# Local attention inside a four-stage block: full-depth score products and block-diagonal values in place of 32 by 32 products

## The chip, the cores and the metric

The kernel runs on one core of a Trainium2 chip. The time is the device time of one execution, in microseconds (us). The kernel before ran three times: 442.93, 444.45 and 447.99 us, median 444.45.

## The reference

The input is 8 batches of 256 tokens with 128 channels. Four stages run one after the other, each adding its result to x: a global causal attention with rotary positions, a feed-forward stage with blockwise FP4 rounding ("a"), the local attention that this change is about, and the feed-forward stage again ("b"). All arithmetic is float32. The local attention, cut to what matters:

```
xn = layernorm(x)                                     # over 128 channels
q, k, v = split(xn @ w_qkv, 3)                        # windows of LS = 32 tokens
q = rmsnorm(q, ln_w);  k = rmsnorm(k, ln_w)           # y * rsqrt(mean(y*y) + 1e-6) * ln_w
att = (q . k) / sqrt(8)                               # 16 heads of 8 channels, inside a window
att = softmax(where(causal, att, -max))
x = x + (att @ v) @ w_proj
```

A batch has 8 windows. Head h = 4g + j owns channels 32g + 8j to 32g + 8j + 7, with g (a group) and j from 0 to 3.

## The kernel before

Five instruction queues (TensorE "PE", VectorE "DVE", ScalarE "ACT", GpSimd "POOL", SyncE "SP" for DMAs) each run one in-order program. Every stage of every batch is written as a Python generator per engine (`front1` to `front3` for the global attention, `ffn1` to `ffn3` with w = `ffn_a` or `ffn_b`, `local1` and `local2` for the local attention). A `yield` ends a step, and the table `TIMES` gives each step its place; `weave` sorts the steps by it, so the order of each engine's instructions is written out beforehand (569 steps on PE, 406 on ACT, 617 on DVE, 119 on POOL, 40 on SP). `FFN_TURNS` says which feed-forward stage may next use the PSUM tile `ffb`. Stages of different batches overlap: while the global attention of one batch runs, the local and feed-forward stages of earlier ones are laid between its steps. Nothing is reordered at run time: an engine whose next instruction waits holds up everything behind it.

PSUM has three tiles: `fb` (four banks) for the global attention, `ffb` (two banks) for the feed-forward stages and `lb` (two banks of 512 float32 columns) for the local attention. So one batch at a time is in `lb`, from its first transpose to its last addition.

The local attention of a batch goes so (lines of the kernel before):

- ACT subtracts the mean (`centre`, L1062); the standard deviation isn't divided out, since the RMS norm removes a common factor from q and k. POOL works out that factor anyway (`deviation`, L1218 and L1220), for the values, and `evl` (L1242), which corrects the small constant of the RMS norm.
- PE transposes the tokens (L780), and multiplies by the weights of q and k (L910) and of v (L913: two products of 128 tokens by 128 channels). The weights of v have their sign turned once at the start (L1054).
- ACT squares and sums q and k (L1123), copies q to SBUF (L1025) and writes the values, scaled, to `Vl` with a column of ones behind each head (L1131). POOL makes the RMS factors `rql` (L1246, L1249). DVE scales k by its factor and the squared norm weights (L1421).
- PE transposes q and k (L780). ACT copies q to `qTl` and writes four copies of k to `Kd`, each with all channels zeroed but those of one j (L1138, a scale from the 0/1 mask `hm`).
- PE adds the causal mask (L927) and makes the scores with 32 products of 32 rows by 32 columns, each with 128 moving columns (L940), half of them in each of two steps.
- DVE takes the row maxima of both banks at once (L1430). PE subtracts them with two products of 512 columns (L946), since one scale per row is all that the exponential can take. ACT takes the exponential, one tile of 128 tokens after the other, with the factor of q as scale (L1149); DVE transposes in 32 by 32 blocks (L1436).
- PE multiplies by the values, 64 products per tile, each 32 rows by 32 columns with 9 moving columns (L960). A float32 product is two PE instructions, each with its own weight load, so this is 128 pairs per tile and 256 per batch. The first of them waits for both exponentials, because the result goes over scores of bank 0.
- DVE divides by the sums (L1440, L1443), PE transposes (L780) and projects (L969), DVE adds to x (L1446).

At the start PE, ACT and DVE wait for `consts_set`, which POOL raises after its last memset (L1203).

## Time and profile before

| | |
|---|---|
| median of 3 runs | 444.45 us |
| the profiled execution | 439.61 us, of which the span from first to last instruction is 437.8 us |
| mean granted TensorE clock | 0.858 of full speed |
| PE busy | 356.9 us, 82% of the span, 5005 matmul instructions |
| DVE busy | 272.3 us, 62% |
| ACT busy | 225.0 us, 51% |
| POOL busy | 149.6 us, 34% |

The busy time of an engine is the time in which at least one of its instructions ran; PE overlaps its matmuls, so a group's busy time is less than its count times the mean of one. PEld is the weight load that goes with each matmul. The granted clock is 1.0 at 2.4 GHz and 0.5 at 1.2 GHz.

### The profile page before, as it was taken

What the parts mean: (1) busy time and instruction counts of PE and PEld (TensorE: products, weight loads), DVE (VectorE), ACT (ScalarE), POOL (GpSimd) and SP (SyncE); (2) the same over time, 40 slices, a digit from 0 to 9 for tenths busy, and PEclk for the clock granted to TensorE, in tenths of its full rate; (3) what the DMA queues carried; (4) which work ended last, traced back from release to release, by engine and by line L of the source; (5) the groups of instructions that cost most, each with busy time, mean ns of one, the idle gap of its engine ahead of it and who ended that gap; (6) DMA issues with size and microseconds to landing.
All of it is one profiled execution on the core that took longest, in us unless ns stands there. A gap on an engine that the chain in (4) does not pass through costs nothing.

```text
span 437.8 us, 12067 instructions
## 1 busy us (share of the span) xinstructions
PE 356.9 (82%) x5005; PEld 236.8 (54%) x5005; DVE 272.3 (62%) x714; ACT 225.0 (51%) x583; POOL 149.6 (34%) x214
## 2 busy tenths in 40 slices
PE   3237799689798898989999999799999878878564
PEld 2124455456664675566566666566755645645333
DVE  2717207549678347867958956856866677654741
ACT  2310343264475348547647873578498476472421
POOL 4130124140451225136413540362460473332313
PEclk9755659599899958989999999779899999899665
DMA  6360062065000615001500150000000000000000
GB/s 180 95 126 0 4 146 72 19 141 86 4 3 3 146 40 108 1 7 36 106 10 18 46 97 4 3 1 3 18 1 1 15 3 1 15 12 3 13 13 12
DMA packets 33114, 17.67 MB, mean 40 GB/s; under 512 B 1874, under 2 KB 32914, under 8 KB 33060
## 3 DMA queue, kind: packets, MB, share of 16 engines
q1 hardware_dynamic: 32772, 16.78, 17.1%
q8 instruction: 39, 0.64, 0.6%
q10 hardware_dynamic: 288, 0.13, 0.1%
q14 instruction: 15, 0.12, 0.1%
HBM read 9.37 MB, written 7.34 MB: 38 GB/s over the span
## 4 chain that ended last, share of the span: by engine, by line
PE 53%; DVE 17%; ACT 12%; issue 7%; POOL 5%; DMA 3%; SPq 2%; DVEq 0%; POOLq 0%; ACTq 0%
PE fb L879 5%; DVE bmax L1371 4%; PE ffb L1011 4%; PE lb L960 4%; PE fb L797 3%; PE ffb L989 3%; PE ffb L993 3%; PE fb L836 3%; PE lb L946 3%; PE fb L867 3%; DMA Kf<-scr_f 3%; PE ffb L1005 2%; PE fb L838 2%; PE fb L869 2%; PE lb L780 2%
## 5 line engine op out<-in xcount | busy, mean ns | idle before, releaser
L1371 DVE TENSOR_REDUCE bmax<-fb 128x3 f32<-128x384 f32 x128 | 66.7, 548 | 27.9 <-PE fb L839 27.3
L1100 ACT ACTIVATE prob<-fb 128x384 f32<-128x384 f32 x128 | 59.5, 492 | 28.9 <-PE fb L870 28.3
L1270 POOL TENSOR_TENSOR fa__w<-fa__w,fa__c 128x704 f32<-128x704 f32 (+1 forms) x10 | 13.7, 1374 | 81.3 <-DVE fa__w L1500 81.3
L836 PE MATMUL fb<-Kf,Qf 48*128 48x256 bf16 x128 | 32.8, 301 | 10.4 <-DVE bmax L1371 4.9
L838 PE MATMUL fb<-maskb 64*128 64x256 bf16 x128 | 32.9, 301 | 0.0
L867 PE MATMUL fb<-Qf,Kf 51*128 51x256 bf16 x128 | 30.6, 298 | 1.2 <-ACT prob L1100 1.0
L879 PE MATMUL fb<-prob,Vf 128*32 128x128 f32 (+1 forms) x512 | 30.0, 356 | 1.1 <-ACT prob L1100 1.0
L869 PE MATMUL fb<-maskb 64*128 64x256 bf16 x128 | 30.3, 294 | 0.0
L960 PE MATMUL lb<-Vl,probT 32*32 32x9 f32 x2048 | 21.7, 175 | 7.0 <-issue 4.6
L836 PEld LDWEIGHTS fb<-Kf,Qf 48*128 48x128 bf16 x128 | 10.8, 95 | 27.9 <-DVE bmax L1371 16.5
L837 PE MATMUL fb<-Kf,Qf 48*128 48x128 bf16 x128 | 25.9, 235 | 0.0
L1270 POOL TENSOR_TENSOR fb__w<-fb__w,fb__c 128x704 f32<-128x704 f32 (+1 forms) x10 | 13.8, 1378 | 35.1 <-DVE fb__w L1500 35.1
L839 PE MATMUL fb<-maskb 64*128 64x128 bf16 x128 | 25.7, 233 | 0.0
L960 PEld LDWEIGHTS lb<-Vl,probT 32*32 32x32 f32 x2048 | 19.8, 107 | 10.8 <-issue 7.8
L868 PE MATMUL fb<-Qf,Kf 51*128 51x128 bf16 x128 | 24.2, 232 | 0.0
L797 PE MATMUL fb<-xnTf,wT 128*128 128x256 f32 x64 | 22.7, 516 | 1.5 <-ACT xnTf L1025 1.5
L870 PE MATMUL fb<-maskb 64*128 64x128 bf16 x128 | 23.8, 228 | 0.0
L879 PEld LDWEIGHTS fb<-prob,Vf 128*32 128x32 f32 x512 | 14.2, 115 | 16.4 <-issue 7.4
L1229 POOL TENSOR_TENSOR qk<-ra,rb 128x512 f32<-128x512 f32 x7 | 8.9, 1269 | 39.2 <-DVE rb L1352 39.2
L1025 ACT ACTIVATE oTf<-fb 128x256 f32<-128x256 f32 x32 | 12.3, 385 | 16.9 <-PE fb L879 16.8
L867 PEld LDWEIGHTS fb<-Qf,Kf 51*128 51x128 bf16 x128 | 10.2, 95 | 19.0 <-issue 10.9
L1011 PE MATMUL ffb<-wdT,fb__hqT 128*128 128x128 f32 (+1 forms) x96 | 17.0, 326 | 3.9 <-ACT fb__hqT L1025 3.9
(202 smaller groups left out, 939.4 us busy)
## 6 DMA issues: line engine op xcount, KB each, us to landing
scr_f<-partsf SPq DMA_DIRECT2D x16, 192.0 KB, 2.4
Qf<-scr_f SPq DMA_DIRECT2D x16, 192.0 KB, 3.8
...
```

The source lines that it names most:

```text
L797: mm = pe.matmul(fb[:, n // 2, (n % 2) * SEQ:(n % 2 + 1) * SEQ], wT[:, n, :], xnTf[:, :], start=True, stop=True)
L836: pe.matmul(S[:, 128:384], Qf[k, g, 128:256], Kf[k, g, 0:256], start=True, stop=True, skip_group_check=True)
L837: pe.matmul(S[:, 0:128], Qf[k, g, 0:128], Kf[k, g, 0:128], start=False, stop=True, skip_group_check=True)
L838: pe.matmul(ends(S, 0, 128), eye_lo[half_, :], twice(m_qk[half_, :]), start=False, stop=True, skip_group_check=True)
L867: pe.matmul(S[:, 128:384], Kf[k, g, 0:128], Qf[k, g, 0:256], start=True, stop=True, skip_group_check=True)
L869: pe.matmul(two(S[:, 0:256], 0, 128), eye_hi[half_, :], twice(m_kq[half_, :]), start=False, stop=True, skip_group_check=True)
L879: mm = pe.matmul(S[32 * j:32 * j + 32, k * P:SEQ], Vfs[b % RING][:, k, h, :], p, start=(k == 0), stop=(k == 1), skip_group_check=True)
L960: mm = pe.matmul(lb[rows, 0, (t * H + h) * VL:(t * H + h + 1) * VL], probT[rows, t, c // 4, c % 4 * LS:(c % 4 + 1) * LS], Vl[rows, t, h, : ...
L1011: mm = pe.matmul(ffb[:, t, 0:D], w.hqT[0:k, t, c, :], wdT[0:k, c, :], start=(c == 0), stop=(c == 2))
L1100: act.activation(prob[:, slot % 8, :], S[:, 0:384], ACT.Exp).then_inc(f.s_exp, 1)
L1270: pool.tensor_tensor(w.w[:, cols], w.w[:, cols], w.c[:, cols], ALU.subtract).then_inc(w.s_hdif, t1 - t0)
L1371: dve.tensor_reduce(bmax[:, h, 1:4], fb[:, h % 2, 0:384].rearrange("p (n k) -> p n k", k=P), AX.X, ALU.max).then_inc(bmax_done, 1)
```

## The change

The score rows are laid out anew: a partition is now (j, query) of one window and a column (window of the tile, g, key), so all 16 heads of a window come out of one product of full depth. Tile t of 128 tokens has bank t of `lb` for its scores and its results.

- ACT writes four masked copies of q (`Qd`, mask `hm`) and four of k (`Kd`, new mask `quarter`, which keeps one group of 32 channels), eight in all in place of one and four.
- PE makes the scores of a window in one product, 128 deep, 128 by 128: 8 per batch in place of 32. Mask, maxima, subtraction, exponential and values go by tile: the second half of the scores doesn't wait behind other work, each tile has its own maxima (two reductions of 512), and the values of tile 0 no longer wait for the exponential of tile 1.
- The values are block-diagonal (`Vd`): row (j, key), four blocks of 9 columns, of which one isn't zero. So 4 groups and 4 windows make 16 products per tile, each 128 deep, 32 by 36: 32 per batch in place of 128. To have the values in rows (j, key), the value projection is 32 products of 32 tokens by 32 channels in place of 2, and ACT writes `Vd` in four masked copies of 256 columns in place of two of 128.
- The layer norm now divides by the deviation: DVE makes a shift (`shl`) and ACT's first step waits for it, which waits for POOL's factor. POOL's `evl` goes. The factor of q moves from the exponential to the copy of q (two ACT instructions in place of one), which now waits for POOL's `rql`.
- At the start ACT's turn of the sign of v goes, and POOL clears `Vd` and sets its ones (one memset of 1152 columns and four of 32 partitions) in place of one small memset.
- `FFN_TURNS` and the whole table `TIMES` are written anew: 577 steps on PE, 414 on ACT, 633 on DVE, as many as before on POOL and SP. In the start, DVE's four steps on the feed-forward weights now come ahead of the rotary products of batch 0, and SP issues one load of x ahead of the first loads of Q and K, not four.

The rest of the kernel is the same line for line. The diff without the tables, the buffers and the launch:

```
-"ident": np.concatenate([eye, (r[:, None] % LS // HD == np.arange(4)[None, :])], 1).astype(np.float32),
+"ident": np.concatenate([eye, r[:, None] % LS // HD == np.arange(4)[None, :], r[:, None] // LS == np.arange(4)[None, :]], 1).astype(np.float32),
...
+Kd = sb("Kd", [P, T * NWIN, GROUPS, LS])
+Qd = sb("Qd", [P, T * NWIN, 4, LS])
+Vd = sb("Vd", [P, T * NWIN, GROUPS, 4, VL])
+nmaxl = sb("nmaxl", [P, T, NWIN * GROUPS])
...
-    for t in range(T):
-        mm = pe.matmul(lb[:, 1, SEQ + t * D:SEQ + (t + 1) * D], xnTl[:, t * P:(t + 1) * P], wqkvb[:, 2 * D:3 * D], start=True, stop=True)
+    wv = wqkvb[:, 2 * D:3 * D].rearrange("p (g j d) -> p j g d", j=4, d=HD)
+    for w in range(T * NWIN):
+        for j in range(4):
+            mm = pe.matmul(lb[j * LS:(j + 1) * LS, 1, SEQ + w * LS:SEQ + (w + 1) * LS], xnTl[:, w * LS:(w + 1) * LS], wv[:, j, :, :],
+                           start=True, stop=True, skip_group_check=True)
     mm.then_inc(l.s_qkv_ps, 1)
...
-    pe.wait_ge(l_kd, b + 1)
-    for i in range(2):
-        pe.matmul(lb[:, i, :], identb, mask_loc.unsqueeze(1).to_broadcast([P, 2, T * P]), start=True, stop=True, skip_group_check=True)
-    for gg in range(2):
-        c0 = gg * T * P
-        if gg:
-            mm.then_inc(l_half, 1)
-            yield
-            pe.wait_ge(l_half, b + 1)
-        for t in range(T):
-            for n in range(NWIN):
-                k0 = t * P + n * LS
-                for i in range(2):
-                    g = 2 * gg + i
-                    rows = slice(32 * g, 32 * g + 32)
-                    mm = pe.matmul(lb[n * LS:(n + 1) * LS, i, c0 + t * P:c0 + (t + 1) * P], qTl[rows, k0:k0 + LS],
-                                   Kd[rows, :, k0:k0 + LS], start=False, stop=True, skip_group_check=True)
-    mm.then_inc(l.s_sc_ps, 1)
-    yield
-    pe.wait_ge(l.s_nmax, b + 1)
-    for i in range(2):
-        mm = pe.matmul(lb[:, i, :], identf, nmaxl[:, 16 * i:16 * i + 16].unsqueeze(2).to_broadcast([P, 16, LS]),
-                       start=False, stop=True, skip_group_check=True)
-    mm.then_inc(l_mx_ps, 1)
-    yield
+    pe.wait_ge(l_qd, b + 1)
     for t in range(T):
         if t:
             yield
-        else:
-            pe.wait_ge(l.s_exp, T * (b + 1))
+        pe.matmul(lb[:, t, :], identb, mask_loc.unsqueeze(1).to_broadcast([P, 2, T * P]), start=True, stop=True, skip_group_check=True)
+        for n in range(NWIN):
+            w = t * NWIN + n
+            mm = pe.matmul(lb[:, t, n * P:(n + 1) * P], Qd[:, w, :, :].rearrange("p j q -> p (j q)"), Kd[:, w, :, :].rearrange("p g k -> p (g k)"),
+                           start=False, stop=True, skip_group_check=True)
+        mm.then_inc(l.s_sc_ps, 1)
+    for t in range(T):
+        yield
+        pe.wait_ge(l.s_nmax, T * b + t + 1)
+        pe.matmul(lb[:, t, :], identf, nmaxl[:, t, :].unsqueeze(2).to_broadcast([P, 16, LS]),
+                  start=False, stop=True, skip_group_check=True).then_inc(l_mx_ps, 1)
+    for t in range(T):
+        yield
         pe.wait_ge(l_probT, T * b + t + 1)
-        for c in range(H):
-            h = 4 * (2 * (c // 4 % 2) + c // 8) + c % 4
+        for g in range(GROUPS):
             for n in range(NWIN):
-                rows = slice(n * LS, (n + 1) * LS)
-                mm = pe.matmul(lb[rows, 0, (t * H + h) * VL:(t * H + h + 1) * VL], probT[rows, t, c // 4, c % 4 * LS:(c % 4 + 1) * LS],
-                               Vl[rows, t, h, :], start=True, stop=True, skip_group_check=True)
+                mm = pe.matmul(lb[n * LS:(n + 1) * LS, t, g * 4 * VL:(g + 1) * 4 * VL], probT[:, t, n, g * LS:(g + 1) * LS],
+                               Vd[:, t * NWIN + n, g, :, :].rearrange("p j e -> p (j e)"), start=True, stop=True, skip_group_check=True)
     mm.then_inc(l.s_o_ps, 1)
...
-    act.wait_ge(lnw_loaded, 48)
-    act.activation(wqkvb[:, 2 * D:3 * D], wqkvb[:, 2 * D:3 * D], ACT.Copy, scale=-1.0)
...
-    centre(l, b, xnl, mvl)
+    act.wait_ge(l_sh, b + 1)
+    for t in range(T):
+        ins = act.activation(xnl[:, t, :], xall[:, b, t, :], ACT.Identity, scale=rsl[:, 1, t:t + 1], bias=shl[:, t:t + 1])
+    ins.then_inc(l.s_xn, 1)
     yield
     act.wait_ge(l.s_xnT_ps, b + 1)
     copy(xnTl[:, :], lb[:, 1, 0:SEQ]).then_inc(l.s_xnT, 1)
...
             ins = act.activation(sql[:, 2 * a + t, :], q4[:, t, a, :], ACT.Square, scale=D ** -0.5,
                                  accum_out=ssl[:, 2 * a + t:2 * a + t + 1])
     ins.then_inc(l_ss, 1)
-    copy(qkn[:, 0, :, :], q4[:, :, 0, :]).then_inc(l_q, 1)
+    yield
+    act.wait_ge(l_rms, b + 1)
+    for t in range(T):
+        ins = act.activation(qkn[:, 0, t, :], q4[:, t, 0, :], ACT.Copy, scale=rql[:, 1, t:t + 1])
+    ins.then_inc(l_q, 1)
     yield
     act.wait_ge(l.s_qkv_ps, 2 * b + 2)
-    act.wait_ge(l.s_rstd, 2 * b + 2)
-    for t in range(T):
-        ins = act.activation(Vl[:, t, :, 0:HD], lb[:, 1, SEQ + t * D:SEQ + (t + 1) * D].rearrange("p (h d) -> p h d", h=H), ACT.Copy,
-                             scale=rsl[:, 1, t:t + 1])
+    v = lb[:, 1, SEQ:2 * SEQ].rearrange("p (n d) -> p n d", d=HD)
+    for j in range(4):
+        ins = act.activation(Vd[:, :, :, j, 0:HD].rearrange("p w g d -> p (w g) d"), v, ACT.Copy, scale=quarter[:, j:j + 1])
     ins.then_inc(l.s_v, 1)
     yield
     act.wait_ge(l_qkT_ps, b + 1)
-    copy(qTl[:, :], lb[:, 1, 0:SEQ])
+    for g in range(GROUPS):
+        act.activation(Kd[:, :, g, :], lb[:, 1, SEQ:2 * SEQ].rearrange("p (w k) -> p w k", k=LS), ACT.Copy, scale=quarter[:, g:g + 1])
     for j in range(4):
-        ins = act.activation(Kd[:, j, :], lb[:, 1, SEQ:2 * SEQ], ACT.Copy, scale=hm[:, j:j + 1])
-    ins.then_inc(l_kd, 1)
+        ins = act.activation(Qd[:, :, j, :], lb[:, 1, 0:SEQ].rearrange("p (w q) -> p w q", q=LS), ACT.Copy, scale=hm[:, j:j + 1])
+    ins.then_inc(l_qd, 1)
     yield
 def local2(b):
     yield
-    act.wait_ge(l_mx_ps, b + 1)
-    s5 = lb[:, :, :].rearrange("p i (g t k) -> p (i g) t k", g=2, t=T)
     for t in range(T):
         if t:
             yield
-        act.activation(probl[:, t, :, :], s5[:, :, t, :], ACT.Exp, scale=rql[:, 1, t:t + 1]).then_inc(l.s_exp, 1)
+        act.wait_ge(l_mx_ps, T * b + t + 1)
+        act.activation(probl[:, t, :, :].rearrange("p n k -> p (n k)"), lb[:, t, :], ACT.Exp).then_inc(l.s_exp, 1)
     yield
     act.wait_ge(l.s_aT_ps, b + 1)
     copy(attnTl[:, :], lb[:, 1, 0:SEQ]).then_inc(l.s_aT, 1)
...
-    pool.memset(Vl[:, :, :, HD:HD + 1], 1.0).then_inc(consts_set, 1)
+    pool.memset(Vd[:, :, :, :, :].rearrange("p w g j e -> p (w g j e)"), 0.0).then_inc(pool_chain, 1)
+    pool.wait_ge(pool_chain, RING + 1)
+    for j in range(4):
+        ins = pool.memset(Vd[j * LS:(j + 1) * LS, :, :, j, HD:VL].rearrange("p w g e -> p (w g) e"), 1.0)
+    ins.then_inc(consts_set, 1)
...
     deviation(b, l, mvl, rsl)
-    pool.tensor_tensor(evl[:, :], rsl[:, 0, :], eps[:, 1, 0:T], ALU.mult).then_inc(l_ev, 1)
     yield
     pool.wait_ge(l_ss, b + 1)
-    pool.wait_ge(l_ev, b + 1)
-    pool.tensor_tensor(rql[:, 0, :].rearrange("p (a t) -> p a t", a=2), ssl[:, :].rearrange("p (a t) -> p a t", a=2),
-                       evl[:, :].unsqueeze(1).to_broadcast([P, 2, T]), ALU.add).then_inc(l_sscale, 1)
+    pool.tensor_tensor(rql[:, 0, :], ssl[:, :], eps[:, 1, :], ALU.add).then_inc(l_sscale, 1)
     pool.wait_ge(l_sscale, b + 1)
     pool.tensor_tensor(rql[:, 1, :], rql[:, 0, :], half[:, :], ALU.pow).then_inc(l_rms, 1)
...
     yield
+    dve.wait_ge(l.s_rstd, 2 * b + 2)
+    if b > 0:
+        dve.wait_ge(l.s_xn, b)
+    dve.scalar_tensor_tensor(out=shl[:, :], in0=mvl[:, :, 0], scalar=-1.0, in1=rsl[:, 1, :], op0=ALU.mult, op1=ALU.mult).then_inc(l_sh, 1)
+    yield
     dve.wait_ge(l_rms, b + 1)
     dve.wait_ge(l_q, b + 1)
     if b == 0:
...
     yield
-    dve.wait_ge(l.s_sc_ps, b + 1)
-    dve.tensor_reduce(nmaxl[:, :], lb[:, :, :].rearrange("p i (n k) -> p (i n) k", k=LS), AX.X, ALU.max, negate=True).then_inc(l.s_nmax, 1)
+    for t in range(T):
+        if t:
+            yield
+        dve.wait_ge(l.s_sc_ps, T * b + t + 1)
+        dve.tensor_reduce(nmaxl[:, t, :], lb[:, t, :].rearrange("p (n k) -> p n k", k=LS), AX.X, ALU.max, negate=True).then_inc(l.s_nmax, 1)
     yield
     for t in range(T):
         if t:
...
     yield
     dve.wait_ge(l.s_o_ps, b + 1)
-    o = lb[:, 0, 0:T * H * VL].rearrange("p (h e) -> p h e", e=VL)
-    link(chain, dve.reciprocal(rdenl[:, :], o[:, :, HD]))
+    o = lb[:, :, 0:H * VL].rearrange("p t (h e) -> p t h e", e=VL)
+    link(chain, dve.reciprocal(rdenl[:, :].rearrange("p (t h) -> p t h", t=T), o[:, :, :, HD]))
     yield
     linked(chain)
-    dve.tensor_tensor(attnl[:, :, :], o[:, :, 0:HD], rdenl[:, :].unsqueeze(2).to_broadcast([P, T * H, HD]), ALU.mult).then_inc(l.s_attn, 1)
+    dve.tensor_tensor(attnl[:, :, :].rearrange("p (t h) d -> p t h d", t=T), o[:, :, :, 0:HD],
+                      rdenl[:, :].rearrange("p (t h) -> p t h", t=T).unsqueeze(3).to_broadcast([P, T, H, HD]), ALU.mult).then_inc(l.s_attn, 1)
     yield
     dve.wait_ge(l.s_proj_ps, b + 1)
```

## Rows read from the trace of the kernel before

**Rows 1.** Page, part 1: busy us (share of span) and instructions.
```profile
PE 356.9 (82%) x5005; PEld 236.8 (54%) x5005; DVE 272.3 (62%) x714; ACT 225.0 (51%) x583; POOL 149.6 (34%) x214
```
**Rows 2.** Windows: length, busy us of PE, PEld, DVE, ACT, POOL; granted clock; DMA.
```profile
120.00:360.00 240.00, 220.71 (x3579) 148.24 (x3574) 169.63 (x456) 151.06 (x409) 93.00 (x130) 0.94 0.14 31
360.00:410.00 50.00, 39.36 (x783) 26.57 (x782) 32.02 (x76) 25.91 (x63) 16.74 (x22) 0.92 0.03 10
410.00:437.80 27.80, 14.78 (x46) 9.83 (x46) 11.06 (x30) 6.94 (x15) 8.30 (x12) 0.56 0.03 10
```
**Rows 3.** Page, part 4: the chain that ended last, by engine.
```profile
PE 53%; DVE 17%; ACT 12%; issue 7%; POOL 5%; DMA 3%; SPq 2%; DVEq 0%; POOLq 0%; ACTq 0%
```
**Rows 4.** Groups of PE: line, tiles, forms, count | busy us, mean ns | idle before.
```profile
L960 PE MATMUL lb<-Vl,probT 32*32 32x9 f32 x2048 | 21.7, 175 | 7.0 <-issue 4.6 <-DVE probT L1436 2.3
...
L913 PE MATMUL lb<-wqkvb,xnTl 128*128 128x128 f32 x32 | 5.0, 279 | 0.0
```
**Rows 5.** Timeline of PE: start us, length us, line, count, idle before.
```profile
147.54 1.25 PE L960 MATMUL lb<-Vl,probT 32*32 32x9 f32 x128
148.72 1.09 PE L886 MATMUL fb<-identhm,oTf 128*128 128x128 f32 x8
...
153.12 1.04 PE L960 MATMUL lb<-Vl,probT 32*32 32x9 f32 x63 [2.00 <-issue]
...
175.55 0.67 PE L940 MATMUL lb<-Kd,qTl 32*32 32x128 f32 x32
176.15 0.28 PE L836 MATMUL fb<-Kf,Qf 48*128 48x256 bf16 x1
...
180.13 0.86 PE L879 MATMUL fb<-prob,Vf 128*32 128x256 f32 x16
180.92 0.28 PE L867 MATMUL fb<-Qf,Kf 51*128 51x256 bf16 x1
...
403.07 1.60 PE L1011 MATMUL ffb<-wdT,fb__hqT 128*128 128x128 f32 x12
404.61 0.55 PE L960 MATMUL lb<-Vl,probT 32*32 32x9 f32 x46
```
**Rows 6.** Windows around the stall at 151 us, columns as in rows 2.
```profile
151.10:153.10 2.00, 0.02 (x3) 0.00 (x0) 0.00 (x0) 0.00 (x0) 0.00 (x0) 0.98 0.50 71
153.50:166.50 13.00, 13.00 (x115) 9.88 (x109) 6.76 (x26) 6.54 (x17) 4.11 (x9) 0.50 0.15 40
```
**Rows 7.** Timeline of ACT in the last batch's local attention.
```profile
385.98 0.40 ACT L1025 ACTIVATE qkn<-lb 128x256 f32<-128x256 f32 x1
386.24 0.65 ACT L1131 ACTIVATE Vl<-lb,rsl 128x128 f32<-128x128 f32 x2
386.74 0.91 ACT L1025 ACTIVATE fb__hqT<-ffb 128x384 f32<-128x384 f32 x2
...
390.02 1.56 ACT L1138 ACTIVATE Kd<-lb,identhm 128x256 f32<-128x256 f32 x4
391.44 0.41 ACT L1025 ACTIVATE fb__xqT<-ffb 128x256 f32<-128x256 f32 x1
```
**Rows 8.** Timeline of all engines, the same batch: maxima, subtraction, exponential.
```profile
396.49 1.23 DVE L1430 TENSOR_REDUCE nmaxl<-lb 128x32 f32<-128x1024 f32 x1 [0.52 <-PE lb L940]
397.77 1.99 PE L946 MATMUL lb<-nmaxl,identhm 128*128 128x512 f32 x4 [0.60 <-DVE nmaxl L1430]
399.79 1.26 ACT L1149 ACTIVATE probl<-lb,rql 128x512 f32<-128x512 f32 x2 [2.12 <-PE lb L946]
```
**Rows 9.** Timeline of all engines at the start.
```profile
3.33 0.95 POOL L1198 MEMSET Vf<- 128x1024 f32 x1
...
4.57 0.15 POOL L1203 MEMSET Vl<- 128x32 f32 x1
4.76 0.49 DVE L1326 BATCH_NORM_STATS2 stf<-xall 128x6 f32<-128x128 f32 x2 [2.73 <-POOL Vl L1203]
...
20.09 0.68 DVE L1363 TENSOR_TENSOR partsf<-restf,partsf 128x512 bf16<-128x512 f32 x1
```

503 lines of the change are left out of this document (246 added, 257 removed), and 97 rows, old and new, of tables (FFN_TURNS, TIMES).

## The prediction, made before the changed kernel ran

> **What bounds the kernel now.** I read part 1 first, for which engine carries the load [rows 1]: PE is busy for 82% of the span, DVE for 62, ACT for 51. Then windows, because such shares are means over stages [rows 2]. From 120 to 360 us PE is busy for 220.7 of 240 us (92%), DVE for 71%, ACT for 63%: here PE bounds. From 360 to 410 us PE has 79% and works for the last two local attentions, which lie one after the other in `lb`: here the length of that chain counts as much. After 410 us only the last feed-forward stage is left. The chain of waits agrees [rows 3]: PE 53%, DVE 17%, ACT 12%, issue 7%.
>
> So the change is worth what it takes from PE in the middle, what it takes from the chain through `lb` near the end, less what its new work on ACT gives back. The sum is made against the profiled execution, 439.61 us; the median of the three runs is 4.84 us (1.1%) above it. I add the sum to the median.
>
> **Part by part, per batch, then times 8.** I price PE by slots: from the start of a burst to the start of the next work behind it. A burst's own length has the latency of its last product in it, and that lies under what follows.
>
> Scores. Before: 64 instructions (32 float32 products) have a slot of 0.60 us for each half, 175.55 to 176.15 [rows 5], with one half in each step; that makes 1.20 us. After: 8 products of full depth, 16 instructions of 128 by 128 with 128 columns. That form stands at L1011, 12 in 1.54 us, 0.128 us each [rows 5], so 2.05 us. The new scores cost 0.85 us more, +6.8 us in all: the small products overlapped in the array, and full ones can't. Mask and subtraction have the same columns as before and cost nothing new.
>
> Values. Before: 128 pairs of load and product in 1.18 us, 147.54 to 148.72 [rows 5], 9.2 ns a pair, twice per batch: 2.36 us. After: 64 pairs, 128 deep, 32 wide, with 36 columns. No row has this form. One neighbour is L960 itself with 9 columns. The other has the new one's depth and width: L879, 16 instructions of which half have 256 and half 128 columns, in 0.79 us, 49 ns each at 192 columns on average [rows 5]. A straight line between 9 and 192 columns gives 15 ns at 36. I take this, 0.97 us, a gain of 1.39 us, -11.1 us in all. Lower end: 9.2 ns, 0.59 us, -14.2. Upper end: no overlap between products, each 36/128 of 0.128 us, so 36 ns, 2.3 us, -0.5.
>
> Value projection. Before 5.0 us in 8 batches, 0.62 us each with about 0.17 us of latency in it [rows 4]. After: 64 pairs with 32 columns; the same line gives 14 ns, 0.91 us, so +0.46 us, +3.7 us in all. Lower end +1.1, upper end (32 ns each) +12.8.
>
> So PE's slots come to -0.6 us, between -6.3 and +19.1. The three quarters fewer value products are mostly paid for by the other two. L879 speaks against the upper end: without overlap its 16 instructions would take 16 x 1.5 x 0.128 = 3.1 us, and they take 0.79.
>
> Stalls inside a burst. The value products are the only matmuls here that use up instructions faster than 10 ns a pair, and the one group with long idle time that nothing but issue ends: 4.6 us of 7.0 [rows 4]. One stall alone is 2.00 us, at 151.1, in the middle of a burst [rows 5], with DVE, ACT and POOL at rest as well [rows 6]. PE's local instructions fall from 2624 to 1184 pairs (2048, 512 and 32 + 32 before; 512, 128 and 512 + 32 after, L910 being the same). I take three quarters of the stalls as gone, -3.5 us; ends 0 and -4.6.
>
> The clock. Behind that stall the granted clock goes to 0.50, the 1.2 GHz level, for 13 us from 153.5, in which PE is never idle [rows 6]; at 2.4 GHz that work would take 6.5 us. I take half, -3.5 us; ends 0 and -6.5, since the first idle time that the new order makes can do the same.
>
> Waits in `lb`. PE's idle time before the values that ends with a DVE transpose is 2.3 us [rows 4]. The values of tile 0 no longer wait for both exponentials; -1.0 us, ends -2.3 and +1.
>
> ACT. A plain copy of 256 columns holds ACT for 0.26 us (385.98 to 386.24), the two value copies for 0.50 (to 386.74), a scaled copy of 256 for 0.355 (four in 1.42 us, 390.02 to 391.44) [rows 7]. Masked q and k: 8 x 0.355 - 0.26 - 1.42 = +1.16 us. Values: 4 x 0.355 - 0.50 = +0.92. q in two scaled pieces: 0.50 - 0.26 = +0.24. The exponential loses its scale operand, at best -0.1. That is +2.2 us a batch, 17.6 us in all. What hides it is the 37% that ACT is idle while PE bounds [rows 2]; if that cover were gone, all 17.6 would show. What does queue behind the steps of 2.84 us (masks) and 1.42 us (values) are exponentials of the global attention, for which PE waits two steps later. I charge ACT's part in the chain and a little for the blocks, 17%: +3.0 us.
>
> DVE. One reduction of 1.23 us [rows 8] becomes two of 512, some 0.7 each, and the shift is a tiny operation of about 0.2: +0.35 us a batch; at DVE's 17% of the chain +0.4 us in all. POOL loses one tiny operation: nothing.
>
> The start. POOL's memset of 1024 columns takes 0.95 us, and DVE's first operation waited for the last one, at 4.57 [rows 9]. 1152 columns take 1.07 us and the small ones follow: `consts_set` is 1.4 us later. But batch 0 goes on only when the third part of q and k is there, at 20.09 us [rows 9], behind the weights' steps on DVE and ACT, which wait for their own DMA; and these are now ahead in DVE's order. I take +0.5, ends -1 and +1.4. SP issues three loads fewer ahead of the first Q and K: nothing, since those wait for the scratch's writes.
>
> The chain through `lb` in the last two batches. Longer: v's four copies stand between q's and the transposes (+1.4 us), three more masked copies (+1.2 us), and ACT's first step waits for POOL and DVE, which the wait for `lb` hides. Shorter: with a tile per bank the second maxima, subtraction and exponential overlap. Before, 1.23, 1.99 and 1.26 us follow one another [rows 8]; after, half of each lies beside the other tile's, some 2.1 us. Net +0.5 us for each batch, +1.0.
>
> Sum: -0.6 - 3.5 - 3.5 - 1.0 + 3.0 + 0.4 + 0.5 + 1.0 = -3.7 us, rounded to -4: 435.6 for a profiled execution, 440.5 for the median. The new order as a whole has no term; I give it 4 us either way.
>
> **The rivals.**
>
> 1. The gain is larger. The pair's spacing stays at 9.2 ns (slots -6.3), all stalls go (-4.6) and so does the slow stretch (-6.5), with -1.0 and +4.9 as above: -13.5, 431 us. For: bursts half as long. Against: the clock is also low where no value product is near, as at the end, 0.56 [rows 2]. Chance 0.20.
> 2. Slower: ACT becomes what the exponentials wait for. Place: ACT's queue between 120 and 360 us, at the masked copies. Price: all of the 17.6 us in place of 3.0, so +10.9, 455 us. It decides once PE finds both score banks full at each such block; ACT's load there goes from 63% to about 70%. Chance 0.15.
> 3. Slower: products of 32 columns have a floor. If 128 x 32 tiles didn't overlap as L879's do, the slots would be +19.1 in place of -0.6: +16, 460 us; the place is L913's and L960's successors. Half way there, 24 ns a pair, gives +9.5 for the slots and 451 us. The row against it is the pair of 9.2 ns, though at a quarter of the depth. Chance 0.10. The Trainium skill, TensorE: Matmul & The Clock Gate, section "Wait — 56ns, not 53.3ns?", says that matmuls never start closer than about 25 ns, however few columns they have; by that rule this rival's half-way case would be the result. The trace of before disagrees at least for 32 x 32 tiles.
> 4. The stalls aren't a matter of how many instructions there are, and the clock falls elsewhere: -3.7 + 3.5 + 3.5 = +3.3, 448 us. That the DMA engines were half busy in the 2 us stall [rows 6] speaks for it, against it that the long stalls lie inside value bursts. Chance 0.13.
>
> **The numbers.** Forecast 0.42, by itself 436 to 445 us. A measurement of this kernel can tell about 1% from no change, 440.0 to 448.9 us. Faster: half of the forecast, all of rival 1, a little of the others, 0.43. Same: the other half, most of rival 4, 0.32. Slower: rivals 2 and 3 and the rest, 0.25. The range reaches to rival 1 and to the half-way case of rival 3: 430 to 452 us.
>
> **What would show it.** Slots of the new value burst near 1.0 us, of the value projection near 0.9, of a tile's four score products near 1.0 (with the mask 1.2). PE's idle time by issue before the values under 1 us. ACT busy near 243 us, DVE near 275, PE near 356. Half-clock stretches fewer between 120 and 400 us. I would be wrong if PE's busy time fell by over 10 us, if ACT's wait ended PE's idle time by over 8 us more than before, or if the new order moved the last local attention by more than the terms above.

## The result, and the profile after

The changed kernel takes 423.01 us (median of 4 runs, 422.21 to 423.25); the kernel before took 443.69 in the same session. The ratio is 0.956, 95% interval 0.949 to 0.964: 20.7 us faster, where 440.5 was forecast, with 430 as the lower end. The profiled execution takes 422.98 us (span 421.1), 16.6 less than that of before. Some executions of a kernel take over 1.5% longer than its fastest; the ratios, and the medians from here on, leave them out (442.9 us for the kernel before).

Part 1 of the page and the chain of waits, to be read beside [rows 1] and [rows 3]:

```profile
PE 337.3 (80%) x3565; PEld 221.1 (53%) x3565; DVE 281.3 (67%) x730; ACT 242.4 (58%) x630; POOL 149.5 (36%) x210
...
PE 42%; DVE 18%; ACT 17%; issue 11%; DMA 5%; SPq 4%; POOL 3%; DVEq 0%; POOLq 0%; ACTq 0%
```

PE is busy for 19.6 us less, where 0.9 was forecast; ACT (242.4) is where it was forecast and DVE (281.3) is 6 us above. PE's share of the chain falls from 53% to 42%, ACT's rises from 12% to 17%. The windows answer to [rows 2]:

```profile
120.00:360.00 240.00, 217.88 (x2551) 144.29 (x2550) 186.22 (x487) 172.75 (x458) 92.67 (x125) 0.96 0.14 30
360.00:410.00 50.00, 32.50 (x298) 21.55 (x296) 28.39 (x79) 23.04 (x60) 15.59 (x22) 0.81 0.03 9
```

In the middle PE is nearly as full as before (91% and 92%), with 2551 matmul instructions in place of 3579. The groups of the three changed products, against [rows 4], and one burst of each with the work that follows it, against [rows 5]:

```profile
L938 PE MATMUL lb<-Kd,Qd 128*128 128x128 f32 x128 | 17.4, 280 | 0.0
...
L951 PE MATMUL lb<-Vd,probT 128*32 128x36 f32 x512 | 7.0, 201 | 1.1 <-DVE probT L1438 1.1
L918 PE MATMUL lb<-wqkvb,xnTl 128*32 128x32 f32 x512 | 6.1, 199 | 0.0
```
```profile
145.36 0.47 PE L951 MATMUL lb<-Vd,probT 128*32 128x36 f32 x32
145.76 0.44 PE L782 MATMUL fb<-identhm,attnf 128*128 128x128 f32 x2
...
207.92 1.05 PE L938 MATMUL lb<-Kd,Qd 128*128 128x128 f32 x8
208.90 0.28 PE L869 MATMUL fb<-Qf,Kf 51*128 51x256 bf16 x1
...
277.59 0.76 PE L918 MATMUL lb<-wqkvb,xnTl 128*32 128x32 f32 x64
278.28 0.86 PE L984 MATMUL ffb<-wguT,fa__xqT 128*128 128x352 f32 x2
```

A tile's 32 value pairs have a slot of 0.40 us, its scores one of 0.9 to 1.0, the 64 pairs of the value projection one of 0.69. The idle time before the values is 1.1 us in all, where [rows 4] had 7.0, and issue ends none of it. No gap of PE over 0.15 us that only issue ends is left anywhere in the trace of after; before had 6.7 us of them. (In the chain, where all engines count, issue rises from 7% to 11%.)

I also read when the global attention of each batch ends (the start, in us, of the DVE addition that closes it), since that work bounds the middle of the kernel. The lower lines are experiments, explained below.

| kernel | batch 0 | 1 | 2 | 3 | 4 | 5 | 6 | 7 |
|---|---|---|---|---|---|---|---|---|
| before | 76.0 | 114.1 | 157.0 | 209.6 | 242.6 | 277.9 | 313.8 | 350.2 |
| after | 77.4 | 108.8 | 147.7 | 186.7 | 227.5 | 262.1 | 298.8 | 333.9 |
| e5 (before, short value bursts) | 74.0 | 112.0 | 152.3 | 202.2 | 233.5 | 269.1 | 303.2 | 339.3 |
| e1 (old work, new order) | 78.7 | 110.2 | 152.2 | 200.5 | 244.7 | 284.6 | 328.2 | 366.6 |
| e9 (the same, short value bursts) | 77.9 | 109.5 | 149.9 | 192.2 | 230.2 | 266.1 | 308.3 | 342.4 |
| e12 (value copies on POOL) | 78.7 | 110.1 | 149.6 | 190.2 | 238.1 | 272.1 | 310.8 | 346.9 |
| e15 (the same, later in POOL's queue) | 77.4 | 108.9 | 147.7 | 186.8 | 224.5 | 259.1 | 297.6 | 333.8 |

From batch 7 to the end both kernels take some 87 us, so the 16 us are won before that. The most is won in batch 3, which takes 52.6 us before and 39.0 after (49.9 in e5, 42.3 in e9); batch 4 gives a part of it back, with 33.0 us before and 40.8 after.

### The profile page after: what moved, and what is told of

Read it like the earlier page. It is cut to its first block, busy times and chain, and to the rows that moved or that the text cites. A ratio compares the mean times of both kernels' runs of the same rounds, so it can differ in the third digit from the quotient of the medians.

```text
span 421.1 us, 9229 instructions
## 1 busy us (share of the span) xinstructions
PE 337.3 (80%) x3565; PEld 221.1 (53%) x3565; DVE 281.3 (67%) x730; ACT 242.4 (58%) x630; POOL 149.5 (36%) x210
## 4 chain that ended last, share of the span: by engine, by line
PE 42%; DVE 18%; ACT 17%; issue 11%; DMA 5%; SPq 4%; POOL 3%; DVEq 0%; POOLq 0%; ACTq 0%
PE fb L881 4%; PE fb L838 4%; PE fb L799 3%; DVE bmax L1365 3%; PE ffb L1002 3%; ACT prob L1088 3%; DMA Kf<-scr_f 3%; PE ffb L980 3%; PE fb L869 2%; PE ffb L984 2%; PE fb L840 2%; PE lb L938 2%; PE ffb L996 2%; PE fb L888 2%; PE lb L944 2%
## 5 line engine op out<-in xcount | busy, mean ns | idle before, releaser
L838 PE MATMUL fb<-Kf,Qf 48*128 48x256 bf16 x128 | 31.3, 300 | 12.2 <-DMA Kf<-scr_f 7.9
L840 PE MATMUL fb<-maskb 64*128 64x256 bf16 x128 | 31.3, 299 | 0.0
L881 PE MATMUL fb<-prob,Vf 128*32 128x128 f32 (+1 forms) x512 | 28.8, 344 | 2.5 <-ACT prob L1088 2.4
L871 PE MATMUL fb<-maskb 64*128 64x256 bf16 x128 | 30.5, 287 | 0.0
L838 PEld LDWEIGHTS fb<-Kf,Qf 48*128 48x128 bf16 x128 | 10.4, 94 | 32.0 <-DVE bmax L1365 16.3
L839 PE MATMUL fb<-Kf,Qf 48*128 48x128 bf16 x128 | 24.7, 234 | 0.0
L841 PE MATMUL fb<-maskb 64*128 64x128 bf16 x128 | 24.4, 232 | 0.0
L872 PE MATMUL fb<-maskb 64*128 64x128 bf16 x128 | 24.1, 224 | 0.0
L799 PE MATMUL fb<-xnTf,wT 128*128 128x256 f32 x64 | 21.7, 498 | 2.1 <-ACT xnTf L1016 2.1
L1227 POOL TENSOR_TENSOR qk<-ra,rb 128x512 f32<-128x512 f32 x7 | 8.9, 1267 | 38.4 <-DVE rb L1346 38.4
L799 PEld LDWEIGHTS fb<-xnTf,wT 128*128 128x128 f32 x64 | 15.5, 253 | 7.1 <-ACT xnTf L1016 4.1
L1002 PEld LDWEIGHTS ffb<-wdT,fb__hqT 128*128 128x128 f32 (+1 forms) x96 | 14.7, 233 | 7.5 <-ACT fb__hqT L1016 6.8
L1016 ACT ACTIVATE oTf<-fb 128x256 f32<-128x256 f32 x32 | 12.2, 381 | 10.5 <-PE fb L881 10.3
```

Source lines behind the costliest of these rows:

```text
L799: mm = pe.matmul(fb[:, n // 2, (n % 2) * SEQ:(n % 2 + 1) * SEQ], wT[:, n, :], xnTf[:, :], start=True, stop=True)
L838: pe.matmul(S[:, 128:384], Qf[k, g, 128:256], Kf[k, g, 0:256], start=True, stop=True, skip_group_check=True)
L839: pe.matmul(S[:, 0:128], Qf[k, g, 0:128], Kf[k, g, 0:128], start=False, stop=True, skip_group_check=True)
L840: pe.matmul(ends(S, 0, 128), eye_lo[half_, :], twice(m_qk[half_, :]), start=False, stop=True, skip_group_check=True)
L841: mm = pe.matmul(ends(S, 64, 64), eye_hi[half_, :], twice(m_qk[half_, 0:64]), start=False, stop=True, skip_group_check=True)
L871: pe.matmul(two(S[:, 0:256], 0, 128), eye_hi[half_, :], twice(m_kq[half_, :]), start=False, stop=True, skip_group_check=True)
```

## The experiments

All times are medians; a ratio is to the kernel before in the same session with its 95% interval. "After" stands at 0.956 [0.949, 0.964]. The median of all runs of the kernel before was 445.9 us in the session of e1 to e4, 444.1 in that of e5 to e8, 443.2 for e9 to e12 and 441.9 for e13 to e15, so ratios of different sessions can differ by 0.9% more than their intervals say. Where two experiments are compared, I give the difference of the medians.

### The order and the work, crossed: e1, e2

e1 is the kernel before with the places of the steps, and the turns of `ffb`, of the kernel after; e2 is the other way round. Steps that one of them lacks are merged with or put behind a neighbour; 5 and 13 steps had to move by a place or more, since the mix would have waited for itself.

```
-TIMES, FFN_TURNS of before      +TIMES, FFN_TURNS of after, two-tile steps merged      (e1)
-TIMES, FFN_TURNS of after       +TIMES, FFN_TURNS of before, new steps 0.1 behind      (e2)
```

> The kernel before, instruction for instruction, but with the new kernel's order of steps and feed-forward turns (the steps that only the new kernel has are left out of the list; 5 of 1950 steps stand one place earlier, so that no engine waits for a step behind the one that waits). Theory A, the gain is in the new local attention's instructions: 437 to 448 us. Theory B, the gain is in the new order of all stages, most of it between 77 and 187 us where the two profiles part: 424 to 431 us. The term for the order in the prediction was 4 us either way.

> The new local attention with the order of steps and the feed-forward turns of the kernel before (its added steps stand right beside the old ones they came from; 13 steps stand one or two places earlier, so that no engine waits for a step behind the one that waits). Theory A, the new instructions carry the gain whatever the order: 423 to 430 us. Theory B, the order carries it: 438 to 446 us. If both parts are needed together, both this run and the old work in the new order are above 436 us.

Measured: e1 467.85 us, ratio 1.046 [1.041, 1.051]; e2 495.93 us, ratio 1.112 [1.104, 1.120]. Both mixes are slower than either theory had them, so the case holds in which both parts are needed together. Each work is best in its own order, by 25 and by 73 us. So the new table is no gain that one can take alone. What in the work it fits is the question of e5, e9, e13 and e14.

### The number of value pairs: e3, e8, e10

These are the kernel after, with each value product cut into pieces. Operands, results and order stay.

```
-                        for n in range(NWIN):
-                            mm = pe.matmul(lb[..., g * 4 * VL:(g + 1) * 4 * VL], probT[...], Vd[:, t * NWIN + n, g, :, :]...)
+                        for j in range(4):           # e3; e8: range(2), 18 columns each; e10: 4 in tile 0, 1 in tile 1
+                            for n in range(NWIN):
+                                mm = pe.matmul(lb[..., (g * 4 + j) * VL:(g * 4 + j + 1) * VL], probT[...], Vd[:, t * NWIN + n, g, j, :], ...)
```

> The new kernel with each value product of 36 columns issued as four products of 9 columns with the same 32-wide weights: as many pairs of load and product per tile (128) as in the kernel before, same result, same order. Theory A1, the number of instructions in a value burst is what cost the time before (long bursts run out of instructions, PE stops, the clock falls): bursts of 1.2 us again, stalls in them, 6 to 15 us slower than the new kernel, 429 to 438 us. Theory A2, only the bursts' own length counts: 2 x 8 x 0.75 us of PE at most, 0 to 6 us slower. Theory B, the order carries the gain: the same as A2.

> The new kernel with each value product issued as two of 18 columns, same result: 64 pairs per tile and 128 per batch, between the new kernel's 32 and 64 and the kernel before's 128 and 256. With four pieces the slots of the group grew by about 20 us, of which some 10 are stalls that came after 200 to 250 pairs close together. If those stalls need that many pairs in a row: no stall of over 0.3 us, only the longer slots, 2 to 7 us slower than the new kernel, 425 to 430 us. If stalls grow in proportion to the pairs: half of the 24 us, 433 to 437 us.

> The kernel after, with the 128 short value pairs of e3 in tile 0 only; tile 1 keeps its 32. The result is the same. By a sum over pairs this is half of e3's extra work, 768 pairs: half of e3's 26 us, 436 us. If what costs is that PE runs out of instructions behind some 200 pairs in a row, a burst of 128 with 32 behind it never gets there: PE has no stall of 2 us inside or behind the values, and the time is the slots alone, 0.8 us a batch, 429 us or less. If one burst of 128 is enough for the stall, 440 or more.

| | pairs per tile | us | ratio |
|---|---|---|---|
| after | 32, 32 | 423.0 | 0.956 [0.949, 0.964] |
| e8 | 64, 64 | 423.9 | 0.962 [0.953, 0.970] |
| e10 | 128, 32 | 429.5 | 0.969 [0.964, 0.974] |
| e3 | 128, 128 | 448.7 | 1.015 [1.009, 1.020] |

The pairs alone take the whole gain away: e3 is as slow as the kernel before, or a little slower, and slower than any of its theories had it. The groups of e8, then of e3, and a part of e3's timeline on PE:

```profile
L952 PE MATMUL lb<-Vd,probT 128*32 128x18 f32 x1024 | 11.4, 187 | 0.8 <-DVE probT L1439 0.4 <-issue 0.3
```
```profile
L952 PE MATMUL lb<-Vd,probT 128*32 128x9 f32 x2048 | 21.5, 179 | 9.6 <-issue 9.4 <-DVE probT L1439 0.2
```
```profile
221.02 2.32 PE L952 MATMUL lb<-Vd,probT 128*32 128x9 f32 x250
225.55 0.24 PE L952 MATMUL lb<-Vd,probT 128*32 128x9 f32 x6 [2.21 <-issue]
225.72 0.87 PE L997 MATMUL ffb<-identhm,fa__hq 128*128 128x128 f32 x6
...
265.65 1.50 PE L881 MATMUL fb<-prob,Vf 128*32 128x256 f32 x15 [2.35 <-issue]
...
347.34 1.83 PE L952 MATMUL lb<-Vd,probT 128*32 128x9 f32 x196
351.31 0.68 PE L952 MATMUL lb<-Vd,probT 128*32 128x9 f32 x60 [2.15 <-issue]
```

Where both tiles' bursts lie one behind the other, PE stops for 2.2 us after 250 pairs, and after 196 in another batch. e3 has seven gaps inside its bursts, 0.3 to 2.2 us long, 9.4 us in all, and two more of 3.6 us together behind a burst (one is the line at 265.65): 13.0 us that only issue ends. A burst of 128 pairs has a slot of 1.19 us in e3, against 0.40 for 32, so 16 bursts cost 12.6 us. The two together are 25.6 of the 26 us. e8, with half the pairs, has two gaps, 0.3 and 0.7 us: its stalls are not half of e3's, and neither is its loss (0.9 us in place of 26, less than its expectation had).

e10 is less clean. PE's timeline of e10, behind a burst and inside one:

```profile
332.04 1.55 PE L954 MATMUL lb<-Vd,probT 128*32 128x9 f32 x160
333.52 0.44 PE L782 MATMUL fb<-identhm,attnf 128*128 128x128 f32 x2
333.79 0.38 PE L999 MATMUL ffb<-identhm,fa__hq 128*128 128x128 f32 x2
335.50 0.33 PE L999 MATMUL ffb<-identhm,fa__hq 128*128 128x128 f32 x1 [1.33 <-issue]
...
395.62 0.32 PE L954 MATMUL lb<-Vd,probT 128*32 128x36 f32 x12 [1.69 <-issue]
```

Its slots cost half of the 12.6 us, 6.3. Its expectation had the time (429 us or less, 429.5 measured), but not the reason: PE does stop, once for 1.7 us after 148 pairs in a row and four times for 0.5 to 1.3 us within 3 us behind a burst, 4.9 us in all. Slots and stops add up to 11.2 us where 6.5 were measured, so a part of the stops doesn't reach the end. The mean granted clock of the profiled runs of after and e3 is the same, 0.92, so the clock doesn't make the difference between these two.

### Short value bursts in the old work: e5, e9

In both orders, the old value products with 16 per tile in place of 64, each with the 36 columns of four heads (for three heads of every four the result is wrong):

```
-                    for c in range(H):
-                        h = 4 * (2 * (c // 4 % 2) + c // 8) + c % 4
+                    for c in range(0, H, 4):
+                        h = 4 * (2 * (c // 4 % 2) + c // 8)
...
-                            ... (t * H + h + 1) * VL], probT[rows, t, c // 4, c % 4 * LS:(c % 4 + 1) * LS], Vl[rows, t, h, :], ...
+                            ... (t * H + h + 4) * VL], probT[rows, t, c // 4, 0:LS], Vl[rows, t, h:h + 4, :]..., ...
```

> The kernel before, in its own order, with 16 value products per tile in place of 64: each is still 32 by 32 but moves the 36 columns of four heads, with the probabilities of the first of them (the other three heads' results are wrong). So it has the new kernel's number of value instructions and columns, and nothing else of it. Theory A, long bursts of value instructions and the stalls in them were the cost: the group's slots fall from about 26 us in all to 7, and most of it reaches the end even in the old order: 424 to 434 us. Theory B, the order decides and gives back only what it was made for: 437 to 446 us.

> The kernel of e1 (the instructions of before in the order of after), but with 16 value products of 36 columns per tile in place of 64 of 9, as in e5 (three heads of every four get a wrong result). With e5, before and e1 this makes a table of two orders by two kinds of value burst. Theory: the new order leaves room for short value bursts only, so the short bursts bring far more here than the 12 us of e5: under 450 us, 20 us or more below e1's 468. Rival: the misfit of e1 lies in the other durations and waits (one maximum over both tiles, the half scores, one masked copy of q), and the short bursts bring their 12 us as in the old order: 456 us or more.

Measured: e5 429.6 us, ratio 0.980 [0.965, 0.995]; e9 436.04 us, ratio 0.989 [0.980, 0.998].

| median us | old order | new order |
|---|---|---|
| old work, 128 value pairs per tile | 442.9 | 467.9 (e1) |
| old work, 32 pairs | 429.6 (e5) | 436.0 (e9) |
| new work, 128 pairs | not run | 448.7 (e3) |
| new work, 32 pairs | 495.9 (e2) | 423.0 (after) |

The short bursts bring 13 us in the old order (9 by the ratio) and 32 in the new one. The groups of e1 and of e9:

```profile
L960 PE MATMUL lb<-Vl,probT 32*32 32x9 f32 x2048 | 23.7, 180 | 16.3 <-issue 9.3 <-ACT probl L1149 6.5 <-DVE probT L1436 0.4
```
```profile
L960 PE MATMUL lb<-Vl,probT 32*32 32x36 f32 x512 | 7.1, 199 | 7.6 <-ACT probl L1149 6.5 <-DVE probT L1436 1.0
```

16.6 us of busy time and all 9.3 us of issue go, 26 of the 32; the wait for the exponential, which tiles of their own end in the kernel after, stays at 6.5. With short bursts the old work gains nothing from the new order (429.6 and 436.0 us, with ratios whose intervals overlap). With long ones it loses 25 us by it; in the new order the bursts of two tiles lie close together, and 9.3 us of issue stand in e1's trace against 6.7 in that of before. PE's waits for ACT are 34.4 us in e1 against 19.4, and they stay in e9 (37.9), so the stops are not the whole of e1's loss.

### The order of the start: e6

The kernel before with after's places for the first stages (43 steps on PE, 42 on DVE, 30 on ACT, 10 on SP differ), the rest as before.

> The kernel before, instruction for instruction, with the new kernel's order for the first stages alone: the weights, the global attention of batches 0 and 1 and its first part of batches 2 and 3, the loads of x, and the first steps of the first feed-forward stage (43 of 569 steps of PE differ, 30 on ACT, 42 on DVE, 10 on SP). No local attention runs there. In the profiles the global attention of batch 1 takes 38.1 us before (76.0 to 114.1) and 31.5 us after (77.4 to 108.8), and so it does in both runs with exchanged orders, by the order. Theory B, the order gains 6 us there by itself: batch 1 ends at 108 to 110 us and the whole is 4 to 7 us faster than before. Theory A (what is gained there is lost again, because the steps behind stand in the old order): batch 1 ends early, the whole within 2 us of before.

Measured: 440.9 us, ratio 0.996 [0.988, 1.003], no difference that can be told. The execution that was traced took 974 us, so this run has no milestones. The global attention of batch 1, with no local work beside it, takes 31.5 us in every kernel with the new order (after, e1, e9) and 38 in those with the old one (before, e5, e2, by the table of milestones and e2's 38.4). So 6.6 us come from the order there. The whole of e6 isn't faster by them: either the old order behind them loses them again or they never came about in e6, which can't be read without its trace.

### ACT's new work: e4, e7, e13, e14

```
+                for g in range(GROUPS):                              # e4: eight more, into tiles that nobody reads
+                    act.activation(Kx[:, :, g, :], lb[:, 1, SEQ:2 * SEQ]..., ACT.Copy, scale=quarter[:, g:g + 1])
+                for j in range(4):
+                    act.activation(Qx[:, :, j, :], lb[:, 1, 0:SEQ]..., ACT.Copy, scale=hm[:, j:j + 1])
...
-                for g in range(GROUPS):                              # Kd, Qd, Vd: 4, 4, 4 copies
+                for g in range(GROUPS if b == 0 else 2):             # e7: 2, 2, 4;  e13, e14: 1, 2, 2
```

> The new kernel with eight more masked copies per batch on ACT, of the same size and source, into two tiles (bfloat16) that nobody reads, ahead of the eight that count: ACT is held 2.8 us longer per batch, 23 us in all, and the chain through lb is that much longer. If ACT's new work is hidden as far as the prediction took it (17% of it shows): 3 to 6 us slower. If it is what now bounds: over 12 us slower. If it costs nothing: within 2 us of the new kernel.

> The new kernel with four of the eight masked copies per batch from batch 1 on (two of k, two of q; the other tiles keep batch 0's content, so the result is wrong). ACT has 1.42 us less per batch, 10 us in all, and the chain through lb is as much shorter. If the new kernel is bound by ACT and this chain throughout: 8 to 13 us faster, 410 to 415 us. If its order hides what it was made for, and only delays show: 0 to 4 us faster, 419 to 423 us.

> The kernel after, in its own order, but from batch 1 on with one of the four masked copies of k, two of q and two of v (the others keep batch 0's data, so the result is wrong): 7 copies of 0.36 us a batch less, which takes ACT's busy time back to that of before, some 225 us. This measures the ACT term of the sum (+3.0 us by the prediction, all 17.6 by its rival 2). By the prediction's 17%: 420 us. By e7 (6.5 us for 10): 411 or 412. If every microsecond of ACT shows: 406.

> The kernel of e2 (the work of after in the order of before, 496 us), with the same 7 copies left out from batch 1 on. Theory: what the old order has no room for is ACT's new work, so the mix loses its price: 450 us or less, 45 us or more below e2, where the same cut in the new order (e13) brings some 12. Rival: the old order is as badly off with the other new steps (a shift and a factor to wait for ahead of the layer norm, a step for each tile): 480 us.

| | ACT busy, us | us | ratio |
|---|---|---|---|
| e4 | 264.6 | 454.5 | 1.018 [1.014, 1.023] |
| after | 242.4 | 423.0 | 0.956 [0.949, 0.964] |
| e7 | 232.6 | 416.6 | 0.947 [0.939, 0.955] |
| e13 | 226.1 | 417.8 | 0.949 [0.942, 0.955] |
| e2, new work in the old order | 244.9 | 495.9 | 1.112 [1.104, 1.120] |
| e14, the same with less ACT | 227.9 | 476.1 | 1.079 [1.068, 1.090] |

The tiles that e7, e13 and e14 leave out keep batch 0's content. Going down, the first 10 us of ACT give 6.5 (4.2 by the ratios) and the next 6.5 nothing; both results lie between the cases of their expectations. Going up, 22 us cost 31, by the medians and between the profiled executions alike. There is no one rate for ACT's work: the order has room for what it was written for, and above it every microsecond and more shows. e4's copies stand ahead of those that count and so lengthen the chain through `lb` as well; load and chain aren't told apart here. In the old order the same 16 to 17 us are worth 20, and the mix stays 33 us slower than before. PE's waits in e14, by what it waited for (total, times, longest):

```profile
PE lb L782 <- ACT xnl L1104: 8.1, 4, 3.6
PE lb L782 <- DVE attnl L1445: 7.0, 4, 2.9
PE ffb L1002 <- ACT fb__hqT L1016: 6.4, 7, 2.8
PE fb L869 <- ACT prob L1088: 5.8, 6, 1.6
```

The largest is the transpose that waits for the scaled layer norm (2.7 us in after, 0.8 before), which now has POOL's factor and DVE's shift ahead of it; that these steps lie too close together in the old order is my reading. My theory for e14 (that ACT's copies are all that doesn't fit) fell; the rival's 480 came within 4 us.

### The value projection: e11

```
-                for w in range(T * NWIN):
-                    for j in range(4):
-                        mm = pe.matmul(lb[j * LS:(j + 1) * LS, 1, SEQ + w * LS:SEQ + (w + 1) * LS], xnTl[:, w * LS:(w + 1) * LS], wv[:, j, :, :], ...)
+                for t in range(T):
+                    mm = pe.matmul(lb[:, 1, SEQ + t * D:SEQ + (t + 1) * D], xnTl[:, t * P:(t + 1) * P], wqkvb[:, 2 * D:3 * D], start=True, stop=True)
```

> The kernel after with the old value projection, two products of 128 by 128 in place of 32 of 32 by 32 (the values then stand in the wrong rows, so the result is wrong). The prediction charged the 32 small products 3.7 us. Their slot after is 0.69 us against some 0.5 for the two, so by slots 1 to 2 us are to be had: 421.5 us. By the prediction's term 419. If the 64 instructions also eat into what PE has in stock, more: 415.

Measured: 417.92 us, ratio 0.945 [0.940, 0.951], some 5 us less than after, between the term of the prediction (3.7) and the dearest case. Its slots are 0.44 to 0.54 us in place of 0.69, 1.6 us in all. The trace doesn't say where the other 3 come from.

### The value copies on POOL: e12, e15

ACT copies v once, POOL writes the four masked copies in one operation, and PE's values wait for it. In e15 that step is 1 to 5 places later in POOL's queue in six of the batches.

```
+                    pool.wait_ge(l.s_v, b + 1)
+                    pool.tensor_tensor(Vd[:, :, :, :, 0:HD]..., vl[:, :]... (each value four times), quarter[:, :]... (each mask along the values), ALU.mult).then_inc(l_vd, 1)
...
-                    for j in range(4):
-                        ins = act.activation(Vd[:, :, :, j, 0:HD]..., v, ACT.Copy, scale=quarter[:, j:j + 1])
+                    copy(vl[:, :], lb[:, 1, SEQ:2 * SEQ]).then_inc(l.s_v, 1)
```

> The kernel after, but ACT copies the values once to SBUF (0.26 us in place of 4 x 0.36) and POOL writes the four masked copies in one operation of 1024 columns (some 2.4 us by the 1.27 us of its 512-column sums), two steps later in its queue; PE's values wait for it. ACT loses about 9 us, POOL gains 19. By e7 (6.5 us for 10 us of ACT) the time falls to 417 or 418. If POOL's block of 2.4 us delays the feed-forward stages or the rotary sums behind it, the gain is eaten: 423 to 428. By the prediction's 17% for ACT's work: 421.5.

> The kernel of e12 (the four masked copies of v on POOL, one operation of 1.9 us), with POOL's new step one to five places later in its queue in six of the batches, so that it no longer stands ahead of the rotary sums (batch 2, where e12 lost most) or of a feed-forward step. ACT's load is the same as in e12. If e12's loss of 14 us against after was the place in the queue: 417 to 420 us, better than after. If it is POOL's 15 us of work or a slower POOL and DVE beside each other: 430 or more.

Measured: e12 435.8 us, ratio 0.986 [0.979, 0.993], slower than every case of its expectation; e15 424.62 us, ratio 0.963 [0.955, 0.971]. e15 lies between its two cases. The load is the same in both (ACT 234.3 and 233.4, POOL 164.3 and 164.5 us). POOL's timeline in e12, and the same stretch in e15:

```profile
191.27 1.26 POOL L1230 TENSOR_TENSOR qk<-ra,rb 128x512 f32<-128x512 f32 x1
195.45 1.89 POOL L1252 TENSOR_TENSOR Vd<-vl,identhm 128x1024 f32<-128x1024 f32 x1 [2.92 <-ACT vl L1020]
197.30 1.15 POOL L1233 TENSOR_TENSOR restf<-qk,partsf 128x512 f32<-128x512 f32 x1
```
```profile
187.81 1.27 POOL L1230 TENSOR_TENSOR qk<-ra,rb 128x512 f32<-128x512 f32 x1
189.85 1.16 POOL L1233 TENSOR_TENSOR restf<-qk,partsf 128x512 f32<-128x512 f32 x1 [0.76 <-ACT partsf L1020]
...
197.31 0.62 POOL L1267 TENSOR_TENSOR fa__xq<-fa__xw,fa__xscale 128x256 f32<-128x256 f32 x1
197.88 1.89 POOL L1252 TENSOR_TENSOR Vd<-vl,identhm 128x1024 f32<-128x1024 f32 x1
```

In e12 POOL waits 2.9 us for ACT's copy with a rotary sum of batch 4 behind it, and by the milestones batch 4 takes 47.9 us, against 37.8 in e15. The waits aren't all of it. The window of 18 us behind them, e12 and then e15, columns as in [rows 2]:

```profile
198.00:216.00 18.00, 14.50 (x83) 8.52 (x83) 10.57 (x21) 7.34 (x18) 4.67 (x8) 0.53 0.00 1
198.00:216.00 18.00, 17.77 (x176) 10.59 (x175) 13.81 (x30) 9.73 (x24) 4.28 (x4) 1.00 0.17 46
```

In e12 the granted clock is at the 1.2 GHz level for nearly all of it, and PE runs 83 matmuls in place of 176. So 11 us (14 between the profiled executions) hung on the place of one step in the queue of an engine that is busy for 38% of the span. A version that beats the kernel after isn't found: 9 us less on ACT bring nothing measurable, as from e7 to e13.

## Why the prediction was wrong

The sum was made against the profiled execution, so its terms are compared with traces: -3.7 us forecast, -16.6 measured.

**PE bounds the middle, and the change pays on PE.** Right, and so was the direction, at 0.43. Of the signs of being wrong that the prediction named, one came: PE's busy time fell by 19.6 us, where over 10 was the mark. PE's idle time that ACT ends rose from 19.4 to 27.4 us, just at its mark of 8.

**The price of the old values. This is the step that failed first.** I took 2.36 us a batch from the cleanest burst, 1.18 us at 147.54, for a gain of 11.1 us, and three quarters of the issue stalls inside the bursts, 3.5: 14.6 us. Added up over the trace, with all idle time in and right behind them left out, the slots of the 16 old bursts come to 20.8 us and those of the new ones to 6.3, a gain of 14.5 us. All 4.6 us of stalls inside the bursts are gone too, and so is a stop of 2.1 us that I had not counted. It stands in a trace of before, one product behind a burst:

```profile
273.60 1.25 PE L960 MATMUL lb<-Vl,probT 32*32 32x9 f32 x128
274.78 0.38 PE L894 MATMUL fb<-wT,attnTf 128*128 128x128 f32 x1
277.26 0.49 PE L894 MATMUL fb<-wT,attnTf 128*128 128x128 f32 x3 [2.11 <-issue]
```

That makes 21.2 us, where I had 14.6. That stalls of issue come from the number of pairs in a row was the right mechanism (e3); the amount was too small. The pairs cost 26 us when they are put back alone (e3) and bring 9 to 13 when they are saved alone in the old order (e5).

**The spacing of the pairs.** Interpolated between L960 and L879 at 15 and 14 ns. Measured 12.5 ns (32 in 0.40 us) and 10.8 ns (64 in 0.69 us). All three slot terms came out better than the value taken: scores +5.2 in place of +6.8 (their slots sum to 15.4 us, before 10.3), value projection +1.1 by the sum of its slots (5.5 against 4.3 without a wait of 0.5) or +1.6 against e11, in place of +3.7. With the values' -14.5 the PE slots are -8.2 us, below my lower end of -6.3, where the sum had -0.6. The line drew its slope from products of 128 and 256 columns; for short ones the columns count for little: 9.3 ns a pair with 9 columns (e3), 10.5 with 18 (e8), 12.5 with 36.

**The clock.** The sign is as forecast, the size isn't shown. The 13 us at 1.2 GHz of [rows 6] are gone (granted clock 1.00 in every 20 us from 120 to 220 us), and others came, 0.74 from 220 to 240. Over the whole run PE is busy for 47.4 us at the 1.2 GHz level after, and for 91.3 before. Windows of before, after and e2, which has the same instructions as after in the old order:

```profile
60.00:360.00 300.00, 271.21 (x4002) 181.43 (x3998) 206.09 (x556) 177.20 (x470) 109.30 (x151) 0.91 0.18 39
60.00:360.00 300.00, 268.58 (x3090) 176.59 (x3088) 224.81 (x596) 202.80 (x534) 113.28 (x151) 0.95 0.19 39
60.00:360.00 300.00, 248.98 (x2581) 163.68 (x2574) 184.38 (x495) 163.49 (x422) 91.56 (x121) 0.85 0.18 38
```

e2 is busy on PE for 371.5 us in all, 34 more than after for the same products, with 139.5 of it at the low level. So busy time isn't work, and a part of the 19.6 us may be the clock's. Against a large term stands that times hardly follow the clock within one kernel: the four runs after have granted clocks from 0.88 to 0.92 and times within 0.25%, and over 39 runs of the kernel before a clock that is 0.04 higher (the distance between the means of the two kernels) goes with some 2.5 us, an estimate from widely scattered runs.

**ACT.** Charged 3.0 us of 17.6; e13 takes 16.3 us of busy time away and gains 5. Near enough, but as a rate, 17%, it was wrong: 65% for the first 10 us (e7, 43% by the ratios), nothing for the rest, and over 100% for work on top (e4). What rival 2 feared begins just above the load that the kernel has, if e4's loss is ACT's load and not its longer chain.

**The start.** +0.5 forecast within -1 to +1.4; batch 0 ends 1.4 us later, DVE's first operation 1.65 us later (6.41 us, behind the memset of `Vd`, before 4.76).

**The waits and the chain in `lb`.** Idle time before the values that a DVE transpose ends fell from 2.3 to 1.1 us, as forecast. A kernel with tiles of their own against one without wasn't tried.

**The order, which had no term.** "4 us either way" was the second failed step. With the slots (-8.2), the stops (-6.7) and ACT (+5), the terms that traces and runs give come to about -10 of the 16.6 us. The remaining 6 (10 against the medians) are the waits, the clock and the order; no run separates them. What is shown is the price of the wrong order: 25 us for the old work (e1) and 73 for the new (e2), where I had bounded it by what nearby waits showed. e6 has the order of the start alone, and it brings nothing by itself.

**The rivals.** 1 (431 us) was nearest, for its reasons: spacing and stalls at their ends. It lacked the longer slots of the other old bursts, the stop behind one, and the order. 3 is out: pairs of load and product of 128 by 32 start 11 to 13 ns apart on average. There the Trainium skill's "TensorE: Matmul & The Clock Gate", section "Wait — 56ns, not 53.3ns?", with some 25 ns between starts, isn't followed by this trace; the products here go to four different column groups. (At the 24 ns of the half-way case the slots come to +8.9 us, not +9.5.) 4 is out by e3: the stalls follow the pairs.

What stays open: what PE waits for in a gap that only issue ends (the trace shows its length and place, the experiments that it follows the number of pairs close together; that the supply of instructions runs dry is my reading), how the last 6 to 10 us divide between waits, clock and order, where 3 of e11's 5 us come from, and how much of the 6.6 us in batch 1 the old work could keep.
